# A graph network on one core: the moving 0/1 rows of the first SAGE product written tile by tile

## The chip, the cores and the metric

One core of a Trainium2 chip runs the whole program. The metric is device time in microseconds (us); lower is better. The engines are PE (TensorE matmuls, with weight loads listed as PEld), DVE (VectorE), ACT (ScalarE), POOL (GpSimd) and SP (SyncE, here mostly the queue that issues DMAs).

## What is computed

Four graph layers run one after the other on 6250 nodes with 128 features and 106250 edges, each on a layer-normed input and added to a residual. Only the first matters here:

```python
def _mean_aggregate(x, src, dst):
    summed = jax.ops.segment_sum(x[src], dst, num_segments=N)
    deg = jax.ops.segment_sum(jnp.ones((src.shape[0],), x.dtype), dst, num_segments=N)
    return summed / jnp.maximum(deg, 1.0)[:, None]

def _sage_conv(x, src, dst, Wl, bl, Wr):
    agg = _mean_aggregate(x, src, dst)
    out = agg @ Wl.T + bl + x @ Wr.T
    nrm = jnp.linalg.norm(out, axis=-1, keepdims=True)
    return out / jnp.maximum(nrm, L2_EPS)
...
h = jnp.maximum(_layernorm(x, axis=-1), 0.0)
x = x + _L0_gnn_ref(h, edge_index, ...)   # _sage_conv, relu, batch norm, _sage_conv
...                                       # a relational layer, a GIN layer, an edge attention layer
```

## The kernel before

The sum over a node's in-edges is written as a product with the adjacency matrix. The matrix is built once, during the first SAGE product, stored to memory as fp8 counts, and loaded again for the second SAGE product and the GIN layer.

The work goes in 13 groups of 512 destination nodes (`DENSE`); the last group has 128. The edges are sorted by destination, so each window of four destination nodes has its edges in one tile of at most 128 edges. For such a tile one matmul of 0/1 rows gives the counts: the stationary operand `by_lo` says for each edge (a partition) which of 128 low source numbers it has, the moving operand `by_key` which of 196 keys (49 source blocks times four destination nodes). A *build* (`build`, L1270) handles four tiles, that is four matmuls of 196 columns (L1280), into PSUM banks 6 and 7, two in each. A group has 32 builds, the last one 8.

DVE writes the rows (`place_one_hots`, L1763): one comparison for `by_lo` (L1771, 128x4 elements) and one for `by_key` (L1772, 196x4 elements) a build, both bf16 with the tile as the innermost dimension. So PE reads every fourth element of either one. There are four buffers of each, and DVE may be four builds ahead (`BUILT_CREDIT` on the semaphore `built`). The codes compared with come from memory, `load_codes(g, s)` on SP's queue into one of two buffers `codes[s]`.

ACT copies the counts of each bank to the fp8 tile of the group (`place_pairs`, L1034 to L1041); PE's next matmuls into a bank wait for that through `placed`:

```python
for h in range(2):
    i = 2 * k + h
    ...
    pe.wait_ge(placed, g * PAIRS_IN_GROUP + i - 1)
    for j in (2 * h, 2 * h + 1):
        last = nc.tensor.matmul(bank[6 + h][:, j % 2 * KEYS:(j % 2 + 1) * KEYS], by_lo[k % 4][:, :, j], by_key[k % 4][:, :, j], start=True, stop=True)
    last.then_inc(built, 1)
```

Group 0 is built by itself, before the layer norm of the input has ended. After that PE multiplies group g (`multiply`, L1357: for each of 49 source blocks three matmuls of 512 columns, L1375, because the input is split into three bf16 parts) while it builds group g+1: build k follows block 47k/32, rounded down (`builds_at`, L1352). At block 24 come eight f32 products with the layer's weights (L1405, L1406), and at the end of a group twelve short matmuls that turn the group's own rows (L1388). DVE does the norms and statistics of earlier groups between its comparisons (`sage`, L2139 to L2162). SP stores each finished group of the matrix and then loads the codes of the group after next (`keep_adjacency`, L573). POOL has nothing to do in this stage; it waits in L770 for its part of the batch norm.

Of the kernel before, what the change touches and what calls it, by code (L numbers as in the profile page):

```python
# [7 lines left out]
BF = mybir.dt.bfloat16  # L8
# [6 lines left out]
P = 128  # L15
# [7 lines left out]
COLS = CHUNKS * P  # L23
# [16 lines left out]
HALO = 48  # L40
# [18 lines left out]
WEIGHT_LOADS = 21  # L59
LATE_LOADS = 4  # L60
# [8 lines left out]
def gnn_stack(nc, x, src, dst, edge_type, Wl1, bl1, Wr1, gamma0, beta0, Wl2, bl2, Wr2,  # L69
# [3 lines left out]
    with ctx:  # L73
        def sb(name, cols, dt=FP, parts=P):
            return ctx.enter_context(nc.sbuf_tensor(name, [parts, cols], dt))

        def sem(name):
            return ctx.enter_context(nc.semaphore(name))
# [46 lines left out]
        neg_row = [sb(f"neg_row{h}", GROUPS + 4) for h in range(2)]  # L125
# [42 lines left out]
        W1s, W2s = sb("W1s", P), sb("W2s", P)  # L168
# [139 lines left out]
        repeats_ready = sem("repeats_ready")  # L308
# [4 lines left out]
        codes_in = [sem(f"codes_in{i}") for i in range(2)]  # L313
        flagged = sem("flagged")
# [218 lines left out]
        def _(sp):  # L533
# [3 lines left out]
            for first in (True, False):  # L537
                for to, of in load_edges(dst, 1, first):
# [12 lines left out]
                      (comp_b[:, :], comp.rearrange("l r n -> (l r n)").partition_broadcast(P)),  # L551
                      (W1s[:, :], W1), (W2s[:, :], W2)]
            loads += [(row, v.partition_broadcast(P)) for row, v in (
                (BL1, bl1), (GA0, gamma0), (BE0, beta0), (ab[:, 0:A5], attn_b), (ab[:, A5:], edge_b))]
            late_loads = [(row, v.partition_broadcast(P)) for row, v in ((BL2, bl2), (B2, b2), (GA2, gamma2), (BE2, beta2))]
            loads += [(to, v.rearrange("(p o) -> p o", o=1)) for to, v in (
# [149 lines left out]
        def _(pool):  # L706
# [485 lines left out]
        def _(pe):  # L1192
# [61 lines left out]
            pe.wait_ge(repeats_ready, 1)  # L1254
# [15 lines left out]
            def build(g, k):  # L1270

                pe.wait_ge(one_hots, g * BUILDS + k + 1)
                for h in range(2):
                    i = 2 * k + h
                    if isinstance(g, int) and g == 0 and i < 2:
                        pass
                    else:
                        pe.wait_ge(placed, g * PAIRS_IN_GROUP + i - 1)
                    for j in (2 * h, 2 * h + 1):
                        last = nc.tensor.matmul(bank[6 + h][:, j % 2 * KEYS:(j % 2 + 1) * KEYS], by_lo[k % 4][:, :, j], by_key[k % 4][:, :, j],  # L1280
                                                start=True, stop=True)
                    last.then_inc(built, 1)
# [358 lines left out]
        def _(dve):  # L1641
# [65 lines left out]
            V.tensor_copy(code, code_f.rearrange("p (d j) -> p d j", j=CODES)).then_inc(ident_done, 1)  # L1707
# [55 lines left out]
            def place_one_hots(g, s, builds, pair):  # L1763

                for k in builds:
# [4 lines left out]
                    of = lambda t: codes[s][:, t, k * CODES:(k + 1) * CODES].unsqueeze(1)  # L1770
                    V.tensor_tensor(by_lo[slot], code[:, 0:P, :], of(0).broadcast_to([P, P, CODES]), ALU.is_equal)  # L1771
                    V.tensor_tensor(by_key[slot], code, of(1).broadcast_to([P, KEYS, CODES]), ALU.is_equal).then_inc(one_hots, 1)  # L1772
# [511 lines left out]
            def relation_counts():  # L2284

                ch(V.tensor_scalar(key_i, ext3[1], 3, None, ALU.logical_shift_left))
                ch(V.tensor_tensor(key_i, key_i, ext3[2], ALU.bitwise_or))
                ch(V.tensor_copy(relation_key, key_i))
                same_as_later(HALO - 1, relation_key, every)
                ch(V.tensor_scalar(repeat[:, 0:4 * P], bank[6][:, :], 1.0, None, ALU.add))  # L2290
                V.tensor_scalar(repeat[:, 4 * P:], bank[7][:, 0:COLS - 4 * P], 1.0, None, ALU.add).then_inc(repeats_ready, 1)
# [307 lines left out]
```

## Time and profile before

| what | before |
|---|---|
| time, median of 3 runs | 5882.75 us (5877.44 to 5894.03) |
| span of the profiled execution | 5889.7 us (the only time given for that execution) |
| PE / PEld / DVE / ACT / POOL busy | 59% / 40% / 40% / 23% / 38% |
| mean granted TensorE clock | 0.726 |
| first SAGE product | from about 251 us to about 939 us |

A row of instructions in order of time gives the start, how long the merged run lasted, the engine, the line, the operation, the written and read tensors, the shape and the count; in brackets, how long the engine had been idle before and what ended that. Matmuls overlap in the pipeline, so the distance from start to start is what one costs in a stream, and its duration is its latency. The granted clock is a share of 2.4 GHz; 0.50 is 1.2 GHz.

### The profile page before, as it was taken

How to read it: one execution, taken by the hardware profiler on the slowest of the kernel's cores; microseconds unless marked ns; L12 is line 12 of the kernel's file. 1: busy time of each engine (PE TensorE's matmuls, PEld its weight loads, DVE VectorE, ACT ScalarE, POOL GpSimd, SP SyncE). 2: the span in 40 equal slices, each digit the busy share in tenths (PEclk: the TensorE clock that was granted, in tenths of full speed). 3: DMA queues.
4: the chain of work that ended last, by engine and by line, in shares of the span. 5: the costliest groups of instructions: out<-in, count | busy, mean ns of one | idle time of the engine just before them, and what ended most of it. 6: DMA issues, size and time to landing. Idle time of an engine off the chain costs nothing.

```text
span 5889.7 us, 68338 instructions
## 1 busy us (share of the span) xinstructions
PE 3488.8 (59%) x18857; PEld 2347.3 (40%) x18858; DVE 2346.7 (40%) x6053; ACT 1356.1 (23%) x2994; POOL 2262.0 (38%) x2340
## 2 busy tenths in 40 slices
PE   5599996998633334333333333337995566566566
PEld 3255553444422223222232332333444455445445
DVE  7756566114322222222122222223116555555556
ACT  2555451001200000000000000001003555555555
POOL 3000001000366666665666666661002444444442
PEclk8699998999756665666555555557996677777767
DMA  2111113222522222222111111113220222122112
GB/s 70 52 68 46 67 45 130 92 87 91 156 56 69 66 68 65 65 69 66 45 46 45 45 45 46 46 43 121 87 109 16 43 45 44 41 43 45 45 41 57
DMA packets 264711, 371.66 MB, mean 63 GB/s; under 512 B 63251, under 2 KB 200250, under 8 KB 256298
## 3 DMA queue, kind: packets, MB, share of 16 engines
q1 hardware_dynamic: 186790, 251.51, 12.8%
q0 software_dynamic: 74464, 114.31, 8.5%
q10 hardware_dynamic: 3364, 4.69, 0.3%
q8 instruction: 47, 0.77, 0.1%
q14 instruction: 46, 0.38, 0.0%
HBM read 261.10 MB, written 109.21 MB: 63 GB/s over the span
## 4 chain that ended last, share of the span: by engine, by line
PE 21%; issue 17%; another core or an unknown queue 13%; DVE 8%; POOL 8%; DVEq 6%; DMA 1%; ACT 1%; ACTq 0%; POOLq 0%; SPq 0%
POOL GS L719 8%; PE psum L1375 7%; PE psum L1535 5%; DVEq L1877 3%; DVE GS L1877 3%; PE psum L1321 3%; PE psum L1562 2%; DMA GS<-xw_table,stage 1%; DVEq L1884 1%; PE psum L1468 1%; PE psum L1469 1%; PE psum L1529 1%; PE psum L1300 1%; DVE O L2514 0%
## 5 line engine op out<-in xcount | busy, mean ns | idle before, releaser
L719 POOL DMA_INDIRECT GS<-xw_table,stage x1664 | 1574.4, 946 | 1444.9 <-issue 1075.0
L1375 PE MATMUL psum<-HA,HT 128*128 128x512 fp8e4 (+1 forms) x5733 | 1251.5, 369 | 54.2 <-DVE HT L2060 54.2
L1321 PE MATMUL psum<-GS 128*128 128x96 f32 x3328 | 688.6, 383 | 652.7 <-DMA GS<-xw_table,stage 576.6
L1321 PEld LDWEIGHTS psum<-GS 128*128 128x128 f32 x3328 | 635.2, 289 | 701.6 <-issue 698.2
L719 POOL DMA_INDIRECT HA<-p_table,stage x624 | 602.1, 965 | 734.4 <-ACT stage L1085 509.2
L1375 PEld LDWEIGHTS psum<-HA,HT 128*128 128x128 bf16 x5733 | 554.0, 100 | 632.5 <-DVE HT L2060 55.2
L1877 DVE TENSOR_SCALAR GS<-iota,HT,wt 128x96 f32<-128x96 f32 x1680 | 473.4, 348 | 454.9 <-issue 453.3
L1891 DVE TENSOR_TENSOR HA<-HA,psum 128x96 f32 x208 | 52.8, 254 | 1388.2 <-remote 964.7
L1300 PE MATMUL psum<-Wcat,HT 128*128 128x512 f32 x196 | 177.1, 1057 | 459.9 <-DVE HT L2349 410.7
L1039 ACT ACTIVATE HA<-psum 128x392 fp8e4<-128x392 f32 x784 | 349.4, 494 | 344.0 <-PE psum L1280 331.2
L815 ACT ACTIVATE stage<-edge_cols 128x16 int32 (+1 forms) x104 | 22.2, 216 | 1551.1 <-PE psum L1321 693.6
L1280 PE MATMUL psum<-edge_cols 128*128 128x196 bf16 x1568 | 340.6, 351 | 44.2 <-ACT HA L1039 23.6
L772 POOL TENSOR_TENSOR HA<-O,sd 128x3200 f32<-128x3200 f32 x1 | 10.1, 10147 | 842.7 <-DVE mu L2321 842.7
L1529 PE MATMUL psum<-HA 128*128 x1696 | 103.4, 174 | 343.9 <-issue 315.4
L1535 PE MATMUL psum<-O,HA 128*128 128x245 f32 x832 | 269.1, 480 | 61.8 <-issue 61.8
L1307 PE MATMUL psum<-ident,HT 128*128 128x128 f32 x49 | 23.1, 472 | 468.6 <-DVE HT L2358 400.0
L1535 PE MATMUL psum<-O 128*128 128x245 f32 x832 | 257.9, 472 | 15.6 <-issue 15.6
L1771 DVE TENSOR_TENSOR edge_cols<-rows,codes 128x512 bf16<-128x512 bf16 x392 | 166.2, 424 | 249.9 <-PE psum L1280 249.5
L1300 PEld LDWEIGHTS psum<-Wcat,HT 128*128 128x128 f32 x196 | 56.5, 318 | 519.0 <-issue 519.0
L1280 PEld LDWEIGHTS psum<-edge_cols 128*128 128x128 bf16 x1568 | 173.4, 115 | 184.6 <-DVE edge_cols L1772 42.7
L1535 PEld LDWEIGHTS psum<-O,HA 128*128 128x128 f32 x832 | 205.3, 257 | 97.6 <-issue 68.1
L2514 DVE TENSOR_TENSOR O<-HA,psum 128x980 f32<-128x980 f32 x208 | 241.9, 1163 | 0.0
(383 smaller groups left out, 4221.3 us busy)
## 6 DMA issues: line engine op xcount, KB each, us to landing
HT<-dst_rows SPq DMA_DIRECT2D x212, 256.0 KB
xw_table<-HT SPq DMA_DIRECT2D x100, 512.0 KB, 3.2
HA<-adj SPq DMA_DIRECT2D x26, 1600.0 KB, 6.4
adj<-HA SPq DMA_DIRECT2D x13, 3136.0 KB, 9.5
HA<-adj SPq DMA_DIRECT2D x26, 1536.0 KB, 9.7
GS<-xw_table,stage POOLq DMA_INDIRECT x1664
HA<-p_table,stage POOLq DMA_INDIRECT x624
h_table<-HA SPq DMA_DIRECT2D x4, 960.0 KB, 5.6
```

The lines of the kernel that those rows point to most:

```text
L719: nc.gpsimd.indirect_dma_start(out=to, out_offset=None, in_=table, in_offset=bass.IndirectOffsetOnAxis(ap=idx, axis=0)).then_inc(done, 16)
L1039: nc.scalar.activation(placed_at[s][:, :, i * 8:i * 8 + 8].rearrange("p b (w d) -> p b w d", d=NODES_IN_TILE), bank[6 + i % 2][:, 0:2 * KE ...
L1280: last = nc.tensor.matmul(bank[6 + h][:, j % 2 * KEYS:(j % 2 + 1) * KEYS], by_lo[k % 4][:, :, j], by_key[k % 4][:, :, j], start=True, stop ...
L1300: nc.tensor.matmul(bank[2 + c][:, :], own, Wcat[1][:, c * 4 * P:(c + 1) * 4 * P], start=True, stop=True)
L1321: last = nc.tensor.matmul(bank[h][:, 0:WINDOW], G3[g][:, j, :], S_pair[h][:, t, :], start=(t == 0), stop=(t == 2 * GT - 1))
L1375: last = nc.tensor.matmul(bank[s][:, 0:w], Hs4[:, b, t, :], adj_tile[s][:, b * GW:b * GW + w], start=(b == 0 and t == 0), stop=(b == SRCS ...
L1529: last = nc.tensor.matmul(bank[4 + u][:, t * B5:(t + 1) * B5], oht_l3[:, g, h, j * P:(j + 1) * P], Qp[:, bass.ds(at[g] * B5 + h * B5, B5)] ...
L1535: return nc.tensor.matmul(bank[2][:, 0:245], lo_l3[u][:, t, :], M_l3[:, t, :], start=False, stop=False, skip_group_check=True)
L1562: last = nc.tensor.matmul(looked_p[j], src_rows[:, j * P:(j + 1) * P], Pp_part[t].rearrange("p (a b) -> p a b", a=A5)[:, :, 0:49], start=( ...
L1771: V.tensor_tensor(by_lo[slot], code[:, 0:P, :], of(0).broadcast_to([P, P, CODES]), ALU.is_equal)
L1877: last = V.tensor_scalar(S_pair[s][:, j, :], iota[:, 0:WINDOW], dl_pair[:, bass.ds(k * 2 * GT + j, 1)], wt[:, bass.ds(k * 2 * GT + j, 1)], ...
L2514: V.tensor_tensor(M_l3[:, at, :].rearrange("p j (d a) -> p j d a", a=A5), hi_l3[:, at, :].unsqueeze(3).broadcast_to([P, GT, 49, A5]), b5[: ...
```

## The change

`by_key` gets the tile as its outer dimension, so that the 196 keys of a tile are contiguous and PE reads the moving operand with step one. `by_lo` stays as it is. For DVE to write this order with runs of four, the key codes are repeated four times each (`spread`); GpSimd does that once for a group (`spread_codes`), and copies the codes for `by_lo` too (`codes_lo`). DVE now waits for GpSimd (`codes_spread`) in place of the DMA; SP waits for it too before it loads the codes two groups ahead, and does this ahead of the store. To find room, `neg_row` shares a tensor with one `spread`, and W1 and W2, whose tensor holds `code_lo` meanwhile, are loaded with the late loads. PE waits for `same_ready` in place of `repeats_ready`.

```diff
-WEIGHT_LOADS = 21
-LATE_LOADS = 4
+WEIGHT_LOADS = 19
+LATE_LOADS = 6
...
-        code = rows[:, 3 * P:3 * P + KEYS * CODES // 2].bitcast(BF).rearrange("p (d j) -> p d j", j=CODES)
+        code = rows[:, 3 * P:3 * P + KEYS // 2].bitcast(BF)
+        code_lo = W12[:, :].bitcast(BF).rearrange("p (d j) -> p d j", j=CODES)
...
-        by_key = [edge_cols[:, 1024 + i * 392:1024 + (i + 1) * 392].bitcast(BF).rearrange("p (d j) -> p d j", j=CODES) for i in range(4)]
+        by_key = [edge_cols[:, 1024 + i * 392:1024 + (i + 1) * 392].bitcast(BF).rearrange("p (j d) -> p j d", j=CODES) for i in range(4)]
+        codes_lo = [rows[:, 6 * P + i * P // 2:6 * P + (i + 1) * P // 2].bitcast(BF) for i in range(2)]
+        spread = [t.bitcast(BF).rearrange("p (w r) -> p w r", r=CODES) for t in (neg_rows[:, 0:2 * P], rows[:, 4 * P:6 * P])]
...
             def keep_adjacency():
                 for g in range(DENSE):
+                    if g + 2 < DENSE:
+                        sp.wait_ge(codes_spread, g + 1)
+                        load_codes(g + 2, g % 2)
                     store_adjacency(g, PAIRS_IN_GROUP if g < FULL_GROUPS else PAIRS_IN_GROUP // 4)
-                    if g + 2 < DENSE:
-                        load_codes(g + 2, g % 2)
...
+            def spread_codes(g):
+
+                s = g % 2
+                pool.wait_ge(codes_in[s], 16 * (g // 2 + 1))
+                if g >= 2:
+                    pool.wait_ge(one_hots, (g - 1) * BUILDS)
+                nc.gpsimd.tensor_copy(codes_lo[s], codes[s][:, 0, :])
+                nc.gpsimd.tensor_copy(spread[s], codes[s][:, 1, :].unsqueeze(2).broadcast_to([P, P, CODES])).then_inc(codes_spread, 1)
+
             align_edges()
             pool.wait_ge(prep_done, 1)
+            spread_codes(0)
             gather_rest(REST_SAGE1, (h_table, P))
+            for g in range(1, DENSE):
+                spread_codes(g)
...
-                        last = nc.tensor.matmul(bank[6 + h][:, j % 2 * KEYS:(j % 2 + 1) * KEYS], by_lo[k % 4][:, :, j], by_key[k % 4][:, :, j],
+                        last = nc.tensor.matmul(bank[6 + h][:, j % 2 * KEYS:(j % 2 + 1) * KEYS], by_lo[k % 4][:, :, j], by_key[k % 4][:, j, :],
...
                     if k == 0:
-                        dve.wait_ge(codes_in[s], 16 * (pair + 1))
+                        dve.wait_ge(codes_spread, g + 1)
...
-                    V.tensor_tensor(by_key[slot], code, of(1).broadcast_to([P, KEYS, CODES]), ALU.is_equal).then_inc(one_hots, 1)
+                    V.tensor_tensor(by_lo[slot], code_lo, codes_lo[s][:, at].unsqueeze(1).broadcast_to([P, P, CODES]), ALU.is_equal)
+                    V.tensor_tensor(in_fours(by_key[slot]),
+                                    code.rearrange("p (d r) -> p d r", r=CODES).unsqueeze(1).broadcast_to([P, CODES, KEYS // CODES, CODES]),
+                                    spread[s][:, at, :].unsqueeze(2).broadcast_to([P, CODES, KEYS // CODES, CODES]),
+                                    ALU.is_equal).then_inc(one_hots, 1)
```

## Rows read from the trace of the kernel before

**Rows 1.** The page: busy time, share of span, instructions of each engine.

```profile
PE 3488.8 (59%) x18857; PEld 2347.3 (40%) x18858; DVE 2346.7 (40%) x6053; ACT 1356.1 (23%) x2994; POOL 2262.0 (38%) x2340
```

**Rows 2.** Windows: length, busy time (count) of PE, PEld, DVE, ACT, POOL; clock; DMA.

```profile
180.00:217.00 37.00, 24.76 (x116) 9.19 (x116) 27.65 (x64) 24.80 (x56) 0.00 (x0) 0.50 0.10 2
252.30:253.50 1.20, 1.20 (x5) 0.42 (x3) 1.20 (x5) 0.89 (x2) 0.00 (x0) 0.50 0.84 341
448.00:930.00 482.00, 471.52 (x2524) 267.43 (x2523) 282.42 (x677) 226.85 (x513) 0.00 (x0) 0.99 0.14 60
```

**Rows 3.** PE in order of time: the short matmuls that end a group.

```profile
306.18 0.83 PE L1388 MATMUL psum<-ident_b,HT 128*128 128x128 bf16 x12
...
590.63 0.83 PE L1388 MATMUL psum<-ident_b,HT 128*128 128x128 bf16 x12
654.26 0.83 PE L1388 MATMUL psum<-ident_b,HT 128*128 128x128 bf16 x12
711.08 0.83 PE L1388 MATMUL psum<-ident_b,HT 128*128 128x128 bf16 x12
774.21 0.83 PE L1388 MATMUL psum<-ident_b,HT 128*128 128x128 bf16 x12
...
887.84 0.83 PE L1388 MATMUL psum<-ident_b,HT 128*128 128x128 bf16 x12
```

**Rows 4.** Waits of ACT, 590 to 600 us: us in total, times, longest.

```profile
ACT HA L1039 <- issue: 6.1, 1, 6.1
```

**Rows 5.** PE in order of time, inside a group.

```profile
618.12 0.87 PE L1280 MATMUL psum<-edge_cols 128*128 128x196 bf16 x4
618.81 1.48 PE L1375 MATMUL psum<-HA,HT 128*128 128x512 fp8e4 x6
620.12 0.87 PE L1280 MATMUL psum<-edge_cols 128*128 128x196 bf16 x4
620.81 0.83 PE L1375 MATMUL psum<-HA,HT 128*128 128x512 fp8e4 x3
621.48 0.87 PE L1280 MATMUL psum<-edge_cols 128*128 128x196 bf16 x4
...
626.88 0.40 PE L1405 MATMUL psum<-WT,GS 128*128 128x128 f32 x2
...
628.69 1.46 PE L1375 MATMUL psum<-HA,HT 128*128 128x512 fp8e4 x6
```

**Rows 6.** ACT in order of time, same stretch.

```profile
618.76 0.89 ACT L1039 ACTIVATE HA<-psum 128x392 fp8e4<-128x392 f32 x2 [0.47 <-PE psum L1280]
```

**Rows 7.** PSUM's matmuls over the whole run: duration min/median/max in ns.

```profile
L1375 PE MATMUL psum<-HA,HT x5733: 219/379/634, 232.6 to 4452.3; 128*128 128x512 fp8e4 x183, 128*128 128x128 fp8e4 x15
L1280 PE MATMUL psum<-edge_cols x1568: 332/355/369, 180.3 to 922.9; 128*128 128x196 bf16 x196
L1388 PE MATMUL psum<-ident_b,HT x441: 219/219/219, 306.2 to 4452.5; 128*128 128x128 bf16 x147
```

**Rows 8.** PSUM's weight loads over the whole run, and one burst in order of time.

```profile
L1540 PEld LDWEIGHTS psum<-HA,HT x1664: 111/118/123, 4594.6 to 5863.2; 128*128 128x128 bf16 x185
...
5246.01 1.32 PEld L1540 LDWEIGHTS psum<-HA,HT 128*128 128x128 bf16 x32
```

**Rows 9.** DVE in order of time: the ends of its three steps between builds.

```profile
591.62 0.75 DVE L2143 SCALAR_TENSOR_TENSOR GS<-psum,keep,O 128x512 f32<-128x512 f32 x1 [1.83 <-PE psum L1388]
...
594.40 0.42 DVE L1771 TENSOR_TENSOR edge_cols<-rows,codes 128x512 bf16<-128x512 bf16 x1
...
613.13 0.68 DVE L2096 TENSOR_TENSOR O<-psum,rows 128x512 f32 x1
...
615.04 0.42 DVE L1771 TENSOR_TENSOR edge_cols<-rows,codes 128x512 bf16<-128x512 bf16 x1
...
626.09 0.56 DVE L1772 TENSOR_TENSOR edge_cols<-rows,codes 128x784 bf16<-128x784 bf16 x1
626.57 0.16 DVE L2124 TENSOR_SCALAR stat<-stat  x1
...
630.48 0.42 DVE L1771 TENSOR_TENSOR edge_cols<-rows,codes 128x512 bf16<-128x512 bf16 x1
```

**Rows 10.** PE in order of time, group 0.

```profile
180.34 0.87 PE L1280 MATMUL psum<-edge_cols 128*128 128x196 bf16 x4 [2.94 <-DVE edge_cols L1772]
181.64 0.86 PE L1280 MATMUL psum<-edge_cols 128*128 128x196 bf16 x4 [0.42 <-ACT HA L1039]
```

**Rows 11.** ACT in order of time, group 0; the second row is the first's second half.

```profile
181.00 0.89 ACT L1039 ACTIVATE HA<-psum 128x392 fp8e4<-128x392 f32 x2 [2.56 <-PE psum L1280]
181.39 0.49 ACT L1039 ACTIVATE HA<-psum 128x392 fp8e4<-128x392 f32 x1
```

**Rows 12.** DVE in order of time, where group 0 begins.

```profile
179.25 0.10 DVE L2281 MEMSET stat<- 128x50 f32 x1
179.39 0.42 DVE L1771 TENSOR_TENSOR edge_cols<-rows,codes 128x512 bf16<-128x512 bf16 x1
179.73 0.56 DVE L1772 TENSOR_TENSOR edge_cols<-rows,codes 128x784 bf16<-128x784 bf16 x1
180.21 0.42 DVE L1771 TENSOR_TENSOR edge_cols<-rows,codes 128x512 bf16<-128x512 bf16 x1
```

**Rows 13.** POOL in order of time: a one-operand and a two-operand instruction.

```profile
1.25 1.51 POOL L711 IOTA edge_cols<- 128x1664 f32 x1
...
964.31 10.15 POOL L772 TENSOR_TENSOR HA<-O,sd 128x3200 f32<-128x3200 f32 x1 [842.65 <-DVE mu L2321]
```

**Rows 14.** PE in order of time, where the first product begins.

```profile
252.33 1.46 PE L1375 MATMUL psum<-HA,HT 128*128 128x512 fp8e4 x3
253.59 0.89 PE L1280 MATMUL psum<-edge_cols 128*128 128x196 bf16 x4
```

**Rows 15.** DVE in order of time, at the start of the run.

```profile
20.23 1.09 DVE L1709 CAST HT<-O 128x896 f32<-128x896 int32 x1 [14.06 <-DMA O<-in_dst]
```

More of the change, by code:

```diff
@@ L124, in gnn_stack @@
         wt = sb("wt", COLS)
-        neg_row = [sb(f"neg_row{h}", GROUPS + 4) for h in range(2)]
+        neg_rows = sb("neg_rows", 4 * P)
+        neg_row = [neg_rows[:, h * (GROUPS + 4):(h + 1) * (GROUPS + 4)] for h in range(2)]
         blk_i = sb("blk_i", GROUPS + 4, I32)
@@ L167, in gnn_stack @@
         Wcat = [sb(f"Wcat{l}", (R + 1) * P) for l in range(2)]
-        W1s, W2s = sb("W1s", P), sb("W2s", P)
+        W12 = sb("W12", 2 * P)
+        W1s, W2s = W12[:, 0:P], W12[:, P:2 * P]
         rows = sb("rows", 7 * P)
@@ L307, in gnn_stack @@
         same_used = sem("same_used")
-        repeats_ready = sem("repeats_ready")
         repeats_t = sem("repeats_t")
@@ L313, in gnn_stack @@
         codes_in = [sem(f"codes_in{i}") for i in range(2)]
+        codes_spread = sem("codes_spread")
         flagged = sem("flagged")
@@ L550, in _ @@
             loads += [(root_s, root.rearrange("l i o -> i l o")),
-                      (comp_b[:, :], comp.rearrange("l r n -> (l r n)").partition_broadcast(P)),
-                      (W1s[:, :], W1), (W2s[:, :], W2)]
+                      (comp_b[:, :], comp.rearrange("l r n -> (l r n)").partition_broadcast(P))]
             loads += [(row, v.partition_broadcast(P)) for row, v in (
@@ L555, in _ @@
             late_loads = [(row, v.partition_broadcast(P)) for row, v in ((BL2, bl2), (B2, b2), (GA2, gamma2), (BE2, beta2))]
+            late_loads += [(W1s, W1), (W2s, W2)]
             loads += [(to, v.rearrange("(p o) -> p o", o=1)) for to, v in (
@@ L1253, in _ @@
             count_same(HALO - 1, 0, CHUNKS, P, 6, 6, 0)
-            pe.wait_ge(repeats_ready, 1)
+            pe.wait_ge(same_ready, HALO)
             for ch in range(CHUNKS):
@@ L1706, in _ @@
             dve.wait_ge(consts, 5)
-            V.tensor_copy(code, code_f.rearrange("p (d j) -> p d j", j=CODES)).then_inc(ident_done, 1)
+            by_code = code_f.rearrange("p (d j) -> p d j", j=CODES)
+            V.tensor_copy(code_lo, by_code[:, 0:P, :])
+            V.tensor_copy(code, by_code[:, :, 0]).then_inc(ident_done, 1)
             dve.wait_ge(dst_deg_in, 16 * EDGE_LOADS)
@@ L1763, in place_one_hots @@
             def place_one_hots(g, s, builds, pair):
+                in_fours = lambda t: t.rearrange("p j (d r) -> p j d r", r=CODES)
                 for k in builds:
                     if k == 0:
-                        dve.wait_ge(codes_in[s], 16 * (pair + 1))
+                        dve.wait_ge(codes_spread, g + 1)
                     dve.wait_ge(built, (g * BUILDS + k) * 2 + 2)
                     slot = k % 4
-                    of = lambda t: codes[s][:, t, k * CODES:(k + 1) * CODES].unsqueeze(1)
-                    V.tensor_tensor(by_lo[slot], code[:, 0:P, :], of(0).broadcast_to([P, P, CODES]), ALU.is_equal)
-                    V.tensor_tensor(by_key[slot], code, of(1).broadcast_to([P, KEYS, CODES]), ALU.is_equal).then_inc(one_hots, 1)
+                    at = slice(k * CODES, (k + 1) * CODES)
+                    V.tensor_tensor(by_lo[slot], code_lo, codes_lo[s][:, at].unsqueeze(1).broadcast_to([P, P, CODES]), ALU.is_equal)
[3 more added lines that the diff above has]
+                                    ALU.is_equal).then_inc(one_hots, 1)
             blk3 = blk_f.rearrange("t (c p) -> t c p", p=P)
@@ L2290, in relation_counts @@
                 ch(V.tensor_scalar(repeat[:, 0:4 * P], bank[6][:, :], 1.0, None, ALU.add))
-                V.tensor_scalar(repeat[:, 4 * P:], bank[7][:, 0:COLS - 4 * P], 1.0, None, ALU.add).then_inc(repeats_ready, 1)
+                V.tensor_scalar(repeat[:, 4 * P:], bank[7][:, 0:COLS - 4 * P], 1.0, None, ALU.add).then_inc(same_ready, 1)
                 dve.wait_ge(repeats_t, 1)
```

## The prediction, made before the changed kernel was run

> **What bounds the kernel now.** I read the profile in this order: the page's busy shares, then the windows of the stage that the change touches, then that stage's instructions in order of time. The page's shares say little by themselves (PE 59%, no engine near full) because they average over stages with different limits [rows 1]. The windows split it: in the bulk of the first SAGE product (448 to 930 us) PE is busy 471.5 of 482 us at a granted clock of 0.99, DVE 282 and ACT 227 [rows 2]. So PE bounds that stage, and what is saved on PE there moves the end. In the stretch before (180 to 217 us, the builds of group 0) PE is busy two thirds of the time (24.8 of 37 us) at clock 0.50: a loop through PE and ACT bounds it, no full engine [rows 2].
>
> The stage runs in groups. The twelve short matmuls that end a group start at 654.26 and 711.08 us, a period of 56.8 us. From 306.18 to 887.84 us ten groups end; eight periods are 56.8 to 57.0, and two (590.63 to 654.26, 711.08 to 774.21) are over 6 us longer [rows 3], because ACT sits 6.1 us on "issue" at the top of the group [rows 4]. Inside a group, triples of 128x512 matmuls alternate with builds of four 128x196 matmuls [rows 5]. Start to start, a build takes 0.69 us, one block's triple 0.67, two blocks' six 1.31. A full group: 147 long matmuls at 0.216 = 31.7, 32 builds at 0.69 = 22.1, the twelve short ones 0.7, the eight f32 products 1.8 (626.88 to 628.69): 56.3 of the 56.8 us [rows 5]. The sum closes, so PE does not wait between them.
>
> **Part 1: the moving read of the builds (L1280).** A build's matmul costs 0.171 us start to start (four in 0.69) for 196 columns, 0.87 ns a column. The long ones cost 0.42 ns a column (six in 1.31) and the short ones, with 128 bf16 columns, 56 ns each: twelve in 0.83, less one duration of 0.219, by eleven [rows 3, 5]. Both of these read the moving operand contiguously; L1280 takes every fourth bf16 of `by_key`. Durations say the same: 219 ns for 128 columns and 379 for 512 put 196 columns at 247 ns, and L1280 has a median of 355 [rows 7]. Its weights are also read at every fourth element, and the change leaves them so. Is it they that cost? L1540 loads weights with the same stride and its 32 loads take 1.32 us; less one of 0.12, by 31, that is 39 ns each [rows 8]. That fits beneath a matmul of 84 ns. So I charge the 0.171 to the moving read alone: contiguous, it should be 196 x 0.43 = 0.084 us, a build 0.34 in place of 0.69, 0.35 less.
>
> The Trainium skill speaks against this. Its page SBUF — State Buffer (section Door 1: The DMA port swizzle, the note on cachelines) says that two accesses to one 16-byte line already give full bandwidth, so up to 8 bf16 can be strided over for free. By that rule the stride of four costs nothing and part 1 gains nothing. The rows above disagree in size: 0.87 against 0.43 ns a column.
>
> **Part 2: what becomes late next, the two PSUM banks.** A build fills banks 6 and 7, two matmuls each; ACT empties each (L1039), and the next build must wait for its bank. Rows give the lags: from a build's start to ACT's start 0.64 us (618.12 to 618.76), that is 0.11 after the second matmul's end; two evacuations in 0.89 with about 0.50 each, so the second starts 0.39 after the first [rows 5, 6]. From ACT's end of the first to PE's next start: in group 0, 181.50 to 181.64, 0.14 (and for the second half I take 0.12, between that 0.14 and the 0.10 from ACT's end at 181.88 to the third matmul at 181.64 + 0.34) [rows 10, 11]. Now place the new build at time 0: first bank computed at 0.084 + 0.247 = 0.33, ACT 0.44 to 0.94, bank free for PE at 1.08; ACT again 0.83 to 1.33, second bank free at 1.45. The next build comes after one block at 0.34 + 0.67 = 1.01: it waits 0.07, and its second half (natural at 1.25) waits until 1.45: 0.27 lost in all. After two blocks (1.65) nothing waits. Of the 31 gaps in a group (build k stands at block 47k/32, rounded down) 17 are of one block, 14 of two; two of the 17 follow another one and lose about 0.06. That is 15 x 0.27 + 2 x 0.06 = 4.2 us a group. Today the same sum has the second bank free at 1.66 and needed at 1.70: no wait, but only just. Bounds of this term: 0 (the lags overlap better) and 8 us (twice the loss).
>
> Sum: a group saves 32 x 0.35 = 11.1, less 4.2, 6.9 us. Eleven groups have 32 builds woven in: 76 us. The one with 8, far apart, saves 8 x 0.35 = 2.8. At the two groups with ACT's 6.1 us pause the build ahead of the pause gains nothing: 0.7 back. About -78 us.
>
> **Part 3: the one-hot rows on DVE (L1771, L1772).** Same counts, same types; `by_key` gets its 784 elements in the order tile, key, with runs of four in the repeated codes as now. Start to start `by_lo` takes 0.34 and `by_key` 0.47 to 0.48 us [rows 9, 12]. I take the same price. The other end is one element per cycle instead of two: the step between the two forms is 0.13 us for 272 elements, so 784 would cost 0.38 more. DVE's work in a group is 32 x 0.82 and 8.6 of the other steps (2.8 from 591.62 to 594.40, 1.9 from 613.13 to 615.04, 3.9 from 626.57 to 630.48), 34.8 us; in a group of 50 it has room, and its longest step between builds, 3.9 us, is shorter than the four builds (about 6 us) that it may be ahead [rows 9]. What GpSimd's copies cost a comparison that runs beside them stands in no row; two copies of 0.7 to 2.0 us together (part 4) in a group, even if DVE stood still for them, fit into its 15 us of room.
>
> **Part 4: GpSimd, queues and the start.** GpSimd gets two copies a group (128 and 512 elements), 26 in all; it is idle for 842 us until 964 [rows 13]. Group g's copies wait for the one-hots of g-2, a whole group ahead of their reader; SP's load of codes g+2 now waits for the copies of g and stands ahead of the store of g, which is earlier than before. Nothing is queued behind those waits that is due. The exception is group 0: DVE builds right after prep_done (179.25 to 179.39, [rows 12]), and now waits for POOL to wake and copy. The IOTA rows give 0.9 ns an element (1664 in 1.51) plus 0.1: 0.7 us for 640; the two-operand row 3.2 ns (3200 in 10.15), 2.0 us [rows 13]. With the wake-up I take 1.5, all on the path, because the loop of 1.28 us a build behind it only starts later; between 0.5 and 3. That loop itself gets no faster: at clock 0.50 the long matmuls too need 1.26/3/512 = 0.82 ns a column [rows 2, 14], about what the strided read takes. The one more copy at the start (`code_lo`) sits before a 14 us wait for the edges [rows 15]; W1 and W2 are loaded later, by two more issues on SP that nothing waits for; that PE waits on `same_ready` in place of `repeats_ready` costs nothing.
>
> **Result.** 5889.7 (the span of the profiled execution; it lies 7 above the median of the runs, 5882.75) less 78 plus 1.5 is 5813 of that execution; against the median **5806 us**.
>
> **Rivals.**
> *A, the forecast*, with part 2's term between half and one and a half times (23 us either way) and POOL between its ends: 5782 to 5831. Chance 0.63.
> *B, no bank loss*: if ACT's lag shrinks with the matmul, a group saves 11.1: 5760. Against it: the loop of 1.28 us in group 0 is made of just these lags. 0.09.
> *C, the moving read isn't the cause* and the change gives PE nothing: POOL costs 1.5: 5884. Against it: L1540's loads and the prices of a column. 0.10. (The Trainium skill's rule in part 1 would end here.)
> *D, `by_key` at one element a cycle*: DVE needs 34.8 + 12 = 47 us a group and its longest step no longer hides as well; a period of 52 us, a little over both engines' work, gives 11 x 4.8 = 53 back in place of 76: 5829. For it: two operands with two repeat levels stand in no row. 0.08.
> *E, slower: the granted clock.* PE's new short waits (4 of 50 us) are the only idle time in this stage; group 0 shows clock 0.50 at two thirds busy. At the lower level a block's triple costs 1.26 instead of 0.65 and a build 0.64, so a group grows by 30 + 10 less the 4 of waits that vanish, 35 us. It decides from a fifth of the stage (6.9/35); at a third: +55, 5937. Against it: 90% busy. 0.04. The rest, 0.06, is spread around.
>
> Out of the range stay C and E: **5758 to 5848** takes in B and D, and nearly the doubled loss of part 2 (+46: 5852). Faster by over 0.3% (about what a measurement of this kernel can tell) 0.85, within 0.3% 0.10 (C), slower 0.05.
>
> **What would show it.** L1280 at about 247 ns and a build at 0.34 us start to start proves part 1; 355 is C. Waits of PE for ACT L1039 of 0.1 to 0.3 us after one-block gaps, and a group of about 50 us, prove part 2; 45.7 is B. L1772's successor at 0.56 us or near 0.94 decides D; clock 0.99 in 448 to 850 us rules out E. The first one-hot should start about 1.5 us later after the last memset of the preparation. The prediction is wrong if the strided weight load, hidden today beneath 171 ns, is what shows at 84.

## The result, and the profile after

The changed kernel took **5792.85 us** (median of four runs, 5783.61 to 5799.9); the kernel before took 5888.39 with one more run beside the three shown (5877.44 to 5895.36). The ratio is 0.9845, 95% interval 0.9818 to 0.9871. That is faster, inside the predicted range, 13 us under the 5806 predicted. The profiled execution spans 5790.6 us against 5889.7.

The page of the kernel after: busy time, share of the span and count for each engine.

```profile
PE 3391.8 (59%) x18857; PEld 2277.1 (39%) x18858; DVE 2350.8 (41%) x6054; ACT 1357.8 (23%) x2994; POOL 2279.8 (39%) x2366
```

PE lost 97 us of busy time and nobody gained much; DVE's 4 us more and POOL's 26 more instructions (18 us) are the price of the change. The shares, 59% for PE in both kernels, would not have told this [rows 1]. The windows do. Kernel after: length, then busy time (count) of PE, PEld, DVE, ACT and POOL, granted clock, DMA share, GB/s.

```profile
180.00:217.00 37.00, 23.71 (x116) 8.69 (x116) 28.60 (x68) 25.40 (x58) 1.15 (x2) 0.50 0.10 2
448.00:840.00 392.00, 377.83 (x2295) 204.32 (x2293) 262.60 (x632) 211.47 (x478) 5.12 (x12) 0.98 0.16 66
```

In the bulk of the first product PE is still the bound (96% busy, clock 0.98), with DVE now at 67% where it was at 59% [rows 2]. In group 0 the clock is 0.50 as before.

PSUM's matmuls of the builds (L1280 is L1298 now) and their weight loads, kernel after, over the whole run: duration min/median/max in ns.

```profile
L1298 PEld LDWEIGHTS psum<-edge_cols x1568: 110/113/152, 180.3 to 840.6; 128*128 128x128 bf16 x196
L1298 PE MATMUL psum<-edge_cols x1568: 245/249/373, 180.3 to 840.7; 128*128 128x196 bf16 x196
```

The median fell from 355 to 249 ns [rows 7]; 247 was forecast. PE in order of time in the kernel after, inside a group: start, time from first start to last end, line, operation, count.

```profile
589.95 1.46 PE L1393 MATMUL psum<-HA,HT 128*128 128x512 fp8e4 x6
591.24 0.51 PE L1298 MATMUL psum<-edge_cols 128*128 128x196 bf16 x4
591.58 0.81 PE L1393 MATMUL psum<-HA,HT 128*128 128x512 fp8e4 x3
592.25 0.75 PE L1298 MATMUL psum<-edge_cols 128*128 128x196 bf16 x4
592.84 1.46 PE L1393 MATMUL psum<-HA,HT 128*128 128x512 fp8e4 x6
594.13 0.51 PE L1298 MATMUL psum<-edge_cols 128*128 128x196 bf16 x4
```

Two kinds of build are to be seen. After six long matmuls (two blocks) a build takes 0.34 us start to start (591.24 to 591.58) where it took 0.69 [rows 5]. After three (one block) it takes 0.59 (592.25 to 592.84): 0.25 of waiting for a bank. One pair of gaps takes 2.89 us (591.24 to 594.13); in the kernel before it takes 3.36 (618.12 to 621.48, [rows 5]).

The short matmuls that end a group (L1388 is L1406 now), kernel after, in order of time:

```profile
298.98 0.83 PE L1406 MATMUL psum<-ident_b,HT 128*128 128x128 bf16 x12
...
447.49 0.83 PE L1406 MATMUL psum<-ident_b,HT 128*128 128x128 bf16 x12
496.91 0.83 PE L1406 MATMUL psum<-ident_b,HT 128*128 128x128 bf16 x12
546.19 0.83 PE L1406 MATMUL psum<-ident_b,HT 128*128 128x128 bf16 x12
603.52 0.83 PE L1406 MATMUL psum<-ident_b,HT 128*128 128x128 bf16 x12
...
856.26 0.33 PE L1406 MATMUL psum<-ident_b,HT 128*128 128x128 bf16 x3
```

The period is 49.4 us (447.49 to 496.91) where it was 56.8 [rows 3]; the two groups with ACT's pause take 57.3 (546.19 to 603.52) and 56.9. Against the kernel before, the first group end comes 7.2 us earlier (298.98 for 306.18), the sixth 44.4 (546.19 for 590.63, [rows 3]), and the last 82.3 (in the kernel before it starts at 938.60).

Waits between 251 and 880 us in the kernel after: us in total, times, longest.

```profile
ACT HA L1057 <- PE psum L1298: 232.7, 337, 6.9
DVE edge_cols L1792 <- PE psum L1298: 160.3, 274, 4.3
PEld psum L1298 <- ACT HA L1057: 79.0, 256, 6.1
```

The third row, weight loads of the builds that wait for ACT to empty a bank, is the new wait: in the kernel before it stood at 32.1 us, 119 times. ACT and DVE still wait for PE far longer than PE for them. So ACT is not the bound by its work; its lag on two banks is.

**What lies behind the first product.** Of the 99.1 us between the two spans 82.3 are gained by its end, and 16.8 after it, where nothing was changed. The last experiment below is about these.

### The profile page after: what moved, and what is told of

It reads as the page before. It is cut to its first block, busy times and chain, and to the rows that moved or that the text cites. A ratio compares the mean times of both kernels' runs of the same rounds, so it can differ in the third digit from the quotient of the medians.

```text
span 5790.6 us, 68377 instructions
## 1 busy us (share of the span) xinstructions
PE 3391.8 (59%) x18857; PEld 2277.1 (39%) x18858; DVE 2350.8 (41%) x6054; ACT 1357.8 (23%) x2994; POOL 2279.8 (39%) x2366
## 3 DMA queue, kind: packets, MB, share of 16 engines
q1 hardware_dynamic: 186790, 251.51, 13.4%
## 4 chain that ended last, share of the span: by engine, by line
PE 21%; issue 17%; POOL 14%; another core or an unknown queue 11%; DVE 6%; DVEq 4%; DMA 2%; ACT 1%; POOLq 0%; ACTq 0%; SPq 0%
POOL GS L725 14%; PE psum L1393 7%; PE psum L1553 5%; PE psum L1339 3%; DVEq L1901 2%; DMA GS<-xw_table,stage 2%; DVE GS L1901 2%; PE psum L1580 1%; PE psum L1318 1%; PE psum L1486 1%; PE psum L1487 1%; DVEq L1908 1%; PE psum L1547 1%; DVE O L2538 1%
## 5 line engine op out<-in xcount | busy, mean ns | idle before, releaser
L1339 PE MATMUL psum<-GS 128*128 128x96 f32 x3328 | 685.8, 381 | 665.2 <-DMA GS<-xw_table,stage 535.2
L1339 PEld LDWEIGHTS psum<-GS 128*128 128x128 f32 x3328 | 632.0, 287 | 715.3 <-issue 712.1
L1393 PEld LDWEIGHTS psum<-HA,HT 128*128 128x128 bf16 x5733 | 539.1, 98 | 591.6 <-DVE HT L2084 55.2
L1547 PE MATMUL psum<-HA 128*128 x1696 | 107.9, 173 | 380.8 <-issue 362.0
L1298 PE MATMUL psum<-edge_cols 128*128 128x196 bf16 x1568 | 242.6, 264 | 49.9 <-ACT HA L1057 24.8
L1318 PEld LDWEIGHTS psum<-Wcat,HT 128*128 128x128 f32 x196 | 56.9, 320 | 538.4 <-issue 538.4
L1547 PEld LDWEIGHTS psum<-HA 128*128 128x128 bf16 x1696 | 85.3, 100 | 421.0 <-issue 405.6
L1792 DVE TENSOR_TENSOR edge_cols<-W,rows 128x512 bf16<-128x512 bf16 x392 | 167.0, 426 | 170.2 <-PE psum L1298 168.6
L839 ACT ACTIVATE HT<-psum 128x512 f32<-128x512 f32 x49 | 29.3, 597 | 864.0 <-PE psum L1319 672.6
```

Source lines behind the costliest of these rows:

```text
L1318: nc.tensor.matmul(bank[2 + c][:, :], own, Wcat[1][:, c * 4 * P:(c + 1) * 4 * P], start=True, stop=True)
L1339: last = nc.tensor.matmul(bank[h][:, 0:WINDOW], G3[g][:, j, :], S_pair[h][:, t, :], start=(t == 0), stop=(t == 2 * GT - 1))
L1393: last = nc.tensor.matmul(bank[s][:, 0:w], Hs4[:, b, t, :], adj_tile[s][:, b * GW:b * GW + w], start=(b == 0 and t == 0), stop=(b == SRCS ...
L1547: last = nc.tensor.matmul(bank[4 + u][:, t * B5:(t + 1) * B5], oht_l3[:, g, h, j * P:(j + 1) * P], Qp[:, bass.ds(at[g] * B5 + h * B5, B5)] ...
L1792: V.tensor_tensor(by_lo[slot], code_lo, codes_lo[s][:, at].unsqueeze(1).broadcast_to([P, P, CODES]), ALU.is_equal)
```

## The experiments

All of them ran on two chips where the kernel before takes 5109.2 and 5108.6 us (the stages behind the first product take less time there), so ratios and stretches are compared, not times. By its time the first comparison ran on a third chip, called the first chip below; the first four experiments ran on one of the other two, the rest on the other.

**Is it the moving read, and it alone?** The kernel before, with nothing changed but the access of L1280's moving operand. It reads each tile's 196 elements of `by_key` in a row as they lie in memory, so the counts are not those of the edges.

```diff
-..., by_key[k % 4][:, :, j],
+..., by_key[k % 4].rearrange("p d j -> p (d j)")[:, j * KEYS:(j + 1) * KEYS],
```

> The kernel before with one edit: each build's matmul reads 196 contiguous elements of the same buffer in place of every fourth one. DVE, GpSimd, SP and all waits are as before; the counts it writes are not those of the edges. Theory 1 (the moving stride is the whole cause): L1280 falls from 355 to about 249 ns, a group from 56.8 to 49.4 us, the end of the first product from 938.6 to about 855 us, and the time by about 83 us, ratio 0.986, as in the changed kernel. Rival (the rest of the change, the codes from GpSimd or the order of the writes, does part of it): the group stays above 50 us and the ratio above 0.99.

Measured: 5024.47 us, ratio 0.9834 (0.9818 to 0.985). Its builds over the whole run (duration min/median/max in ns) and two of them in order of time:

```profile
L1280 PE MATMUL psum<-edge_cols x1568: 245/249/373, 174.4 to 833.6; 128*128 128x196 bf16 x196
```

```profile
498.42 0.51 PE L1280 MATMUL psum<-edge_cols 128*128 128x196 bf16 x4
498.76 0.81 PE L1375 MATMUL psum<-HA,HT 128*128 128x512 fp8e4 x3
499.43 0.75 PE L1280 MATMUL psum<-edge_cols 128*128 128x196 bf16 x4
500.01 1.46 PE L1375 MATMUL psum<-HA,HT 128*128 128x512 fp8e4 x6
```

The same 249 ns, the same 0.34 us for a build, the same 0.25 of waiting behind a one-block gap, a group of 49.4 us. The access of one operand is the whole gain; the new layout on DVE, GpSimd's copies and the moved loads give nothing by themselves. The ratio of the kernel after on such a chip, 0.9839 (0.9824 to 0.9854), is not to be told from this one.

**How does the price go with the step?** The same line of the kernel before, read at every second element and at every third (4 and 6 bytes apart; every fourth, 8 bytes, is the kernel before). Again the counts are not those of the edges.

```diff
-..., by_key[k % 4][:, :, j],
+..., by_key[k % 4].rearrange("p d j -> p (d j)")[:, 0:392:2],    # one run
+..., by_key[k % 4].rearrange("p d j -> p (d j)")[:, 0:588:3],    # the other
```

> The kernel before, each build's matmul reads every second element of the buffer (4 bytes apart) in place of every fourth (8 bytes); the counts are not those of the edges. If a stride costs because each access fetches 8 bytes and uses one element of them, a step of 4 bytes leaves two a fetch: 249 ns and 84 ns start to start as contiguous, group 49.4 us, ratio 0.986. If any step over one halves the rate: 355 ns, 171 ns, group 56.8, ratio 1.000. Between (each access pays in proportion): about 300 ns and a group near 53 us.

> The kernel before, with the moving rows of the builds read at every third bf16 element (6 bytes apart) in place of every fourth; the counts are then not those of the edges. Steps of 1 and of 2 elements measured 84 and about 88 ns a matmul and a duration of 245 and 247 ns, a step of 4 171 ns and 355. Theory (the read has a width in bytes, 4 bytes of it per column's time, and beyond that the price goes up with the step): 0.128 us a matmul, duration about 300 ns, a build 0.51 us, a group of about 52 us, ratio about 0.99. Rival 1 (one step in price, and every step above 2 pays it whole): 0.171 us, 355 ns, group 56.8, ratio 1.0. Rival 2 (only a step of 4 collides, as banks would make it): 0.085 us, 247 ns, group 49.4, ratio 0.984.

Measured: step 2, 5027.73 us, ratio 0.9842 (0.9826 to 0.9859); step 3, 5061.2 us, ratio 0.9908 (0.9893 to 0.9923). The builds over the whole run, step 2 and then step 3:

```profile
L1280 PE MATMUL psum<-edge_cols x1568: 247/251/369, 173.8 to 833.9; 128*128 128x196 bf16 x196
```

```profile
L1280 PE MATMUL psum<-edge_cols x1568: 291/297/372, 174.4 to 867.0; 128*128 128x196 bf16 x196
```

A build without a wait, in order of time, again step 2 and then step 3:

```profile
495.82 0.52 PE L1280 MATMUL psum<-edge_cols 128*128 128x196 bf16 x4
496.18 0.81 PE L1375 MATMUL psum<-HA,HT 128*128 128x512 fp8e4 x3
```

```profile
491.76 0.69 PE L1280 MATMUL psum<-edge_cols 128*128 128x196 bf16 x4
492.29 0.81 PE L1375 MATMUL psum<-HA,HT 128*128 128x512 fp8e4 x3
```

| step | build, us | ns a column (build / 4 / 196) | ns a byte of the step |
|---|---|---|---|
| 1 (after) | 0.34 | 0.43 | |
| 2 | 0.36 | 0.46 | 0.115 |
| 3 | 0.53 | 0.68 | 0.113 |
| 4 (before) | 0.69 | 0.88 | 0.110 |

So from 4 to 8 bytes the price of a column is nearly in proportion to the bytes stepped over; at 4 bytes it is almost that of a column read contiguously (0.46 for 0.43). Longer steps were not run. The group at step 3 takes 52.3 us (52 expected). Both rivals, one jump in price above step 2 and a collision only at step 4, are out. (The 245 and 247 ns in the text above are the shortest durations of steps 1 and 2; the medians are 249 and 251.) The Trainium skill (page SBUF — State Buffer, section Door 1: The DMA port swizzle) lets 8 bf16 be strided over for free, because two accesses to a 16-byte line are enough; the runs disagree for this operand, at 8 bytes with 0.88 ns a column for 0.43, and even at 6.

**Does the weight load show?** The prediction named this as what would break it. The kernel after, with its weights read contiguously too (its counts are then not those of the edges).

```diff
-..., by_lo[k % 4][:, :, j], by_key[k % 4][:, j, :],
+..., by_lo[k % 4].rearrange("p d j -> p (d j)")[:, j * P:(j + 1) * P], by_key[k % 4][:, j, :],
```

> The changed kernel, and the weights of the builds are read contiguously too (128 elements in a row of the same buffer); the counts are not those of the edges. Theory 1 (weights at a stride are hidden beneath an 84 ns matmul): build start to start stays 0.34 us, group 49.4, time within 3 us of the changed kernel, ratio to before 0.985. Rival (the strided weight load now shows, above all behind a wait for a bank): each of 17 waiting builds a group shorter by up to 0.02 to 0.1 us, 4 to 18 us in all, ratio down to 0.982.

Measured: 5025.49 us, ratio 0.9837 (0.9821 to 0.9854), beside 0.9839 (0.9824 to 0.9854) of the kernel after on the other chip. The loads, over the whole run:

```profile
L1298 PEld LDWEIGHTS psum<-edge_cols x1568: 94/98/153, 175.0 to 832.4; 128*128 128x128 bf16 x196
```

A load takes 98 ns in place of 113, the group 49.1 us in place of 49.4: 0.3 us a group, about 3 us over the product. The time itself is not to be told from that of the kernel after. It is the builds that wait for a bank that are shorter, 0.48 us for 0.50 (groups from 391.13 here and from 398.08 in the kernel after, where the rest of a wait falls ahead of the build), and the others stay at 0.34: that is the rival's mechanism at its smallest size, 0.02 a waiting build. But for that the strided weights are hidden under matmuls of 84 ns.

**Are the bank waits what is late next?** The kernel after with the builds spread evenly over the 147 long matmuls instead of over whole blocks, so that four or five long matmuls stand between any two in place of three or six. Nothing else changes.

```diff
-                return [k for k in range(count) if k * (SRCS - 2) // count == b]
+                return [k for k in range(count) if k * PARTS * (SRCS - 2) // count + PARTS - 1 == b]
...
-                        if q == TO_SAGE1 and not is_block(g, FULL_GROUPS):
-                            for k in builds_at(g, b):
-                                build(g + 1, k)
+                            if q == TO_SAGE1 and not is_block(g, FULL_GROUPS):
+                                for k in builds_at(g, b * PARTS + t):
+                                    build(g + 1, k)
```

> The changed kernel with the builds spread by matmul and not by block: build k stands behind matmul 141k/32 + 2 of the group, so gaps are 4 or 5 long matmuls in place of 3 or 6. Theory 1 (about 3.8 us a group are lost on one-block gaps, where the bank isn't free for 1.26 us after a build's start, while 1.01 would do): a gap of 4 needs 0.86 + 0.34 = 1.20, loses 0.06, one of 5 nothing; 19 x 0.06 = 1.1 us lost, group 46.8 us, 11 x 2.6 = 29 us less than the changed kernel, ratio to before about 0.980. Rival (something else sets the pace between builds, ACT's or DVE's own rate): group stays 49.4, ratio 0.985; if DVE falls behind, PE waits for DVE L1793 and it is above that.

Measured: 4989.3 us (4987.27 to 4989.53), ratio **0.9764** (0.9748 to 0.9781). PE inside a group, the ends of two groups, and the wait for the banks (251 to 840 us: total, times, longest):

```profile
432.14 0.50 PE L1298 MATMUL psum<-edge_cols 128*128 128x196 bf16 x4
432.48 1.24 PE L1393 MATMUL psum<-HA,HT 128*128 128x512 fp8e4 x5
433.56 0.51 PE L1298 MATMUL psum<-edge_cols 128*128 128x196 bf16 x4
433.90 1.02 PE L1393 MATMUL psum<-HA,HT 128*128 128x512 fp8e4 x4
434.76 0.56 PE L1298 MATMUL psum<-edge_cols 128*128 128x196 bf16 x4
435.16 1.24 PE L1393 MATMUL psum<-HA,HT 128*128 128x512 fp8e4 x5
```

```profile
428.37 0.83 PE L1406 MATMUL psum<-ident_b,HT 128*128 128x128 bf16 x12
474.31 0.83 PE L1406 MATMUL psum<-ident_b,HT 128*128 128x128 bf16 x12
```

```profile
PEld psum L1298 <- ACT HA L1057: 14.8, 16, 6.2
```

The wait falls from 79.0 to 14.8 us, most of it at ACT's two pauses, and the group to 45.9, 3.5 less than in the kernel after. Expected were 46.8 and 29 us less in all; the ratios put it at about 38. With no wait at all it would be 147 x 0.216 + 32 x 0.34 + 0.7 + 1.8 = 45.1. After four long matmuls many builds still take up to 0.06 more (434.76 to 435.16, 0.40), about 0.8 us a group, which closes the sum. This version beats both kernels: of the 11.2 us a group that the read could give, the change left a third in the order of the builds.

**GpSimd's start.** The spread kernel with group 0's copies moved ahead of GpSimd's wait for the preparation: they need only their codes.

```diff
-            pool.wait_ge(prep_done, 1)
             spread_codes(0)
+            pool.wait_ge(prep_done, 1)
```

> The kernel after with its builds spread by matmul (as in the run that spread them) and group 0's GpSimd copies ahead of the wait for the preparation. Theory: the first one-hot starts 0.1 to 0.2 us after the last memset of the preparation in place of 1.1, all of it on the path, so 1 us less than the spread kernel alone up to the first group end; the copies of group 1 may then run beside the first one-hots of group 0 or before them, and the 0.5 us that DVE lost beside them goes or stays with that. In total time about 0.976 of the kernel before, not to be told from the spread kernel alone (1 us of 5000). Rival: the start of group 0 is set by something else (PE's or ACT's first instructions), and the first group end stays where it was.

First the kernel after, DVE and then POOL in order of time where group 0 begins:

```profile
178.24 0.10 DVE L2305 MEMSET stat<- 128x50 f32 x1
179.35 0.43 DVE L1792 TENSOR_TENSOR edge_cols<-W,rows 128x512 bf16<-128x512 bf16 x1 [1.00 <-DVE stat L2305]
...
180.60 0.97 DVE L1793 TENSOR_TENSOR edge_cols<-rows,neg_rows 128x784 bf16<-128x784 bf16 x1
```

```profile
178.41 0.29 POOL L777 COPY rows<-codes 128x128 bf16<-128x128 bf16 x1 [56.77 <-DVE stat L2305]
178.65 0.60 POOL L778 COPY neg_rows<-codes 128x512 bf16<-128x512 bf16 x1
179.72 0.68 POOL L777 COPY rows<-codes 128x128 bf16<-128x128 bf16 x1 [0.46 <-issue]
180.35 0.80 POOL L778 COPY rows<-codes 128x512 bf16<-128x512 bf16 x1
```

Memset to first one-hot is 1.11 us (178.24 to 179.35) where it was 0.14 [rows 12]: 1.0 for the two copies. Group 1's two copies then run beside DVE's comparisons, and both engines are longer at it: 0.68 and 0.80 for 0.29 and 0.60, 0.97 for 0.56. The same in the run with the copies moved (DVE, then POOL):

```profile
172.73 0.51 DVE L2301 CAST pair_i<-lo_pair 128x112 int32<-128x112 f32 x1
173.32 0.10 DVE L2305 MEMSET stat<- 128x50 f32 x1
173.45 0.42 DVE L1792 TENSOR_TENSOR edge_cols<-W,rows 128x512 bf16<-128x512 bf16 x1
```

```profile
172.56 0.61 POOL L778 COPY neg_rows<-codes 128x512 bf16<-128x512 bf16 x1
```

Measured: 4987.45 us (4986.56 to 4988.16), ratio 0.9763 (0.975 to 0.9777): by the times not to be told from the spread kernel. In the traces the first one-hot stands 0.13 after the memset, as expected. But the copies now meet the CAST, which takes 0.51 in place of 0.22, and the memset stands 0.8 later than in the spread kernel's trace (173.32 for 172.56, on two chips). So group 0 starts only 0.2 earlier (173.45 for 173.66), and the product 0.3 (245.53 for 245.81).

The first group end comes 1.1 earlier (289.46 for 290.54). That is the size expected, but not for the reason expected: 0.8 of it arises inside the first group, from the clock. Windows from where the product begins, the spread kernel and then this run, columns as in the windows above:

```profile
245.50:251.50 6.00, 6.00 (x25) 3.14 (x23) 4.49 (x11) 2.66 (x6) 0.00 (x0) 0.57 0.44 180
```

```profile
245.50:251.50 6.00, 6.00 (x30) 3.22 (x29) 4.77 (x13) 3.11 (x8) 0.00 (x0) 0.73 0.36 146
```

A mean of 0.57 is 0.50 for 5.2 of the 6 us, one of 0.73 for 3.2: the clock rises 1.9 us earlier, 1.7 of it counted from the product's start, and half of these 1.7 is saved. The last group end stands at 812.05 for 813.75; the other 0.6 of these 1.7 us lies in the two groups with ACT's pause (54.07 and 53.60 us for 54.47 and 53.82), where the clock also rises sooner after PE's restart. So the run shows the gap gone, and 0.3 us of it at the product's start; the rest of the 1.7 is the clock's.

**The 16.8 us behind the first product.** Both kernels once more on one chip, unchanged.

> The kernel before once more, for its trace on the same chip as the next ones. Theory: what the change gives after the first product (some 17 us of the 99 between the two profiled spans) is not its doing but differs from execution to execution, so the time from the end of the first product to the end of the span should come out different by 5 to 20 us between executions of the same kernel. Rival: those 17 us belong to the change; then this length is the same to 2 us in two traces of the kernel before, and about 17 us longer than in the traces of the kernel after.

> The kernel after once more. The first product should take the same time to 1 us as in the first trace of it (from the first group end to the last, 557.3 us), and about 82 us less than in the kernel before up to its end. Theory: the length behind the first product differs between executions of this same kernel by 5 to 20 us. Rival: it is fixed, and shorter than in the kernel before by some 17 us in every trace.

Measured: kernel before 5107.42 us; kernel after 5026.22 (5025.84 to 5026.79), ratio 0.9839 (0.9824 to 0.9854). Where the gathering passes (L1321, L1339 after) and a line of the last stage (L1529, L1547 after) begin and end, kernel before and then after:

```profile
L1321 PE MATMUL psum<-GS x3328: 248/421/501, 1551.6 to 3649.7; 128*128 128x96 f32 x196
```

```profile
L1339 PE MATMUL psum<-GS x3328: 247/421/501, 1470.7 to 3569.0; 128*128 128x96 f32 x196
```

The passes take 2098.1 and 2098.3 us: the same, and the last matmul of L1529 starts 1425.0 behind their end in both (5074.7, and 4994.0 in L1547). Between the last group end and the passes the kernel after takes 1.0 us more (619.4 for 618.4), as it does on the first chip. So on this chip the change gives nothing behind the first product, and its 82.4 us (5108.61 less 5026.22) are those of the first product (933.18 to 851.23 at its last group end, 82.0). On the first chip the same stretches are 2455.7 and 2448.7 us for the passes, 1846.1 and 1835.5 behind them. Both texts expected something else: the rival, a gain of 17 us in every trace, is refuted; but that the length differs by 5 to 20 us between executions is not what this chip shows either, where the two kernels agree to 0.2 in these stretches, and where all eight traces of the two chips have 4172.1 to 4174.9 us from the last group end to the end of the span, whatever the kernel. It would have to be the first chip's, whose runs of one kernel spread over 16 to 18 us where this one's spread over 1 to 3. No run there tells it, so it stays open.

## Why the prediction was right, and where its terms were off

**Mechanism.** The read of the moving operand at step four was the price, and the stage is PE's: shown by the first experiment, which has the kernel before's timing of everything but that read and gives the whole gain. Duration (249 for 247 ns) and build (0.34 us) are as forecast.

**Part 2, the bank waits, held.** The forecast was 0.27 lost behind a one-block gap; measured 0.25. Per group the forecast was 4.2 and a net of 6.9; the normal groups save 7.45 (five of them from 306.18 to 590.63, now 298.98 to 546.19: 37.2 / 5), so the loss is 11.2 - 7.45 = 3.75, about 15 x 0.25. The term was 0.45 too large: 15 x 0.02 of that is the lags, put together from rows of two decimals, and the rest is the rounding of the 0.35. The two builds that follow another one-block gap lose what was forecast (0.39 and 0.40 us for 0.34, in the group from 447.49). Over eight normal groups: +4.4 us.

**The pause groups** saved 6.3 and 6.2 where 6.55 was forecast. The prediction saw one build without gain (0.35). The rows show a second thing, the clock. One window behind the pause, of the kernel before and then of the kernel after, same columns as above:

```profile
601.40:603.40 2.00, 2.00 (x9) 0.80 (x7) 0.90 (x2) 0.87 (x2) 0.00 (x0) 0.67 0.00 0
```

```profile
557.00:559.40 2.40, 2.40 (x8) 0.82 (x7) 0.90 (x2) 0.77 (x2) 0.00 (x0) 0.53 0.00 0
```

Behind the 5 to 6 us in which PE stands still the granted clock is the lower level, 1.2 GHz. It rises at about 602.7 us in the kernel before (a mean of 0.67 is 0.50 for two thirds of the window) and at 559.3 in the kernel after: 4.0 us after PE's restart at 598.73, and 5.0 after that at 554.25. Half of the 1.0 between them is lost: 0.5. PE's standstill is itself 0.34 longer (5.60 for 5.26), and the two builds at the lower clock take 0.70 and 0.66 us where they took 0.74 and 0.71, a gain of 0.1 for 0.7, less a bank wait of 0.25 that isn't there: 0.35. Together 1.2, which is what these groups gain less than the others (7.45 less 6.3 and 6.2). In the second pause group the rise comes 3.0 and 4.2 us after the restart, in the second traces of the two kernels 4.3 and 3.3, and 5.4 and 4.5; over all ten traces it lies between 2.8 and 5.4. Why it comes when it does no run here tells. It is the clock of rival E, in its smallest form.

**Part 3.** The two comparisons cost 0.426 and 0.560 us in the mean, for 0.424 and 0.559 before; DVE's steps are hidden and D is out.

**Part 4 and the first group.** 1.5 us forecast; measured 1.0, the gap ahead of the first one-hot. The row that was missing, what a copy costs a comparison beside it, is now there (0.97 for 0.56), but it does not reach the end of group 0: from the first one-hot to the last one's end the kernel after takes 36.94 us (179.35 to 216.29), and the first experiment, which has no copies, 36.89 (173.44 to 210.33).

Two other things at the start went the other way. From the first build of group 0 to its last it is 39.24 us where it was 39.96, 1.27 us a build for 1.29. The forecast had "no faster" there; the first experiment has 39.18 with nothing changed but the read, so these 0.7 us are the read's too. And the last memset of the preparation came 1.0 us earlier (178.24 for 179.25), 0.9 on the second chip. I did not forecast that. In four traces in which all of the program ahead of it is that of the kernel before it stands from 172.72 to 173.46, so most of it can be scatter; its cause stays open. Together the product's first long matmul stands 0.8 us earlier (251.51 for 252.33), where the forecast had it 1.5 later.

The first group then takes 6.4 us less, under the 7.45 of the normal ones, and the clock is the reason again. Six us from about the product's start, of the kernel before and of the kernel after:

```profile
252.00:258.00 6.00, 6.00 (x29) 3.19 (x28) 4.58 (x12) 2.96 (x7) 0.00 (x0) 0.79 0.38 146
```

```profile
251.50:257.50 6.00, 6.00 (x29) 3.26 (x27) 4.53 (x12) 2.98 (x7) 0.00 (x0) 0.67 0.36 146
```

The clock is at the lower level until 254.5 in the one and 255.5 in the other, 2.2 and 4.0 us after that first long matmul, and half of the 1.7 between is lost. The same holds between the first experiment and the second trace of the kernel after, whose last group end is 2.1 us later (851.23 and 849.11): 0.3 of that stands at the product's start, 1.0 arises in the first group and 0.8 in the two pause groups, each time with a later rise of the clock. So the 2.1 us are not the price of GpSimd's copies.

**Together.** Forecast at the end of the first product 76.5; measured 82.3. Normal groups +4.4, pause groups -0.6, start and first group +1.8 (7.2 for 6.9 - 1.5, which is +2.3 for the start and -0.5 for the group), last group +0.1: 5.7 of the 5.8. The rest of the distance to 5806 is what lies behind the first product on the first chip, and that the two medians of the kernel before differ by 5.6 (5882.75 and 5888.39). By the medians the change is worth 95.5 us, of which 13 lie behind the first product, are no part of the forecast's mechanism, and stay unexplained. That the time is only 13.4 under the forecast is 5.8 + 13.2 - 5.6: the nearness of the total proves less than the 82.3 us for 76.5 at the end of the product.

**The rivals.** B (no bank loss) had the group at 45.7, which is what the spread builds give (45.9) and not the change. C and D are refuted by the builds' 0.34 us and by DVE's durations, E by the clock of 0.98.

## What to carry to other kernels

Compare matmuls by nanoseconds a column, start to start, over all lines of a kernel: the one line whose price is twice that of the others has a reason in its access, and a strided moving operand is one that the kernel can change. Before counting the saving in full, lay the faster loop against the lag of what empties its banks: here that sum found both the third of the gain that was lost and the order of the builds that brings it back. And put a helper engine's first piece of work, which a whole stage waits for, ahead of that engine's waits for anything it does not need; here that took away a gap of 1.0 us, and brought the product's start 0.3 us forward, which is within the scatter of that start. Before a difference of 1 or 2 us between two traces is put down to an edit, compare when the granted clock rises in each: here that alone moved 1 to 2 us.

## What the runs showed of the hardware that I had not expected

- The price of the moving read is no jump but a line: 0.46, 0.68 and 0.88 ns a column at 4, 6 and 8 bytes a step, so step two is nearly free (0.36 us a build for 0.34). At the lower clock step four is nearly free too: behind the pause a build takes 0.74 and 0.71 us with it and 0.70 and 0.66 contiguously, where at the upper level it is 0.69 for 0.34.
- A weight load read at every fourth element takes 113 ns for 98, and 15 ns more is nearly all hidden.
- A GpSimd copy beside DVE's two-operand comparison lengthens both (0.80 for 0.60 us, 0.97 for 0.56), and beside DVE's CAST of 112 elements the CAST (0.51 for 0.22).
- After a stand of 5 to 6 us, or at the start of the product, the granted clock goes from 0.50 to 1.00 at a moment that differs from trace to trace (2.2 to 4.9 us after the product's first long matmul in the ten traces). A block's triple takes 1.26 us at the lower level for 0.67, so each us there costs about half a us.
- Two chips ran the kernel before within 1 us of each other, the first comparison's runs took 15% longer (5888 for 5109); of these 779 us only 5 stand at the end of the first product (938.60 for 933.18).
